# Row maxima of an attention kernel from the high halves alone, two heads at a time in the two halves of the TensorE array

## The reference, cut to what matters

```python
x = L0_attn_x                                   # (4, 1024, 128), float32
x = x + _layernorm(_L0_attn_ref(_layernorm(x), wq, wk, wv, wo))
x = x + _layernorm(_L0_ffn_ref(_layernorm(x), ...))
# _L0_attn_ref, 16 heads of 64:
q, k, v = (einsum('btd,od->bto', x, w) for w in (wq, wk, wv))     # split into heads
q, k = apply_rotary_emb(q, cos, sin), apply_rotary_emb(k, cos, sin)
scores = einsum('bhid,bhjd->bhij', q, k) * 64 ** -0.5
scores = where(causal, scores, -inf)
out = einsum('bhij,bhjd->bhid', softmax(scores), v)
out = einsum('btd,od->bto', out, wo)
```

## Time and profile before

| | |
|---|---|
| median of three runs | 1312.89 us (1311.67 to 1315.08) |
| the profiled execution: its own time, its span | 1314.52 us, 1312.8 us |
| busy in its span: TensorE, VectorE, GpSimd, ScalarE | 1152.0, 994.7, 956.3, 932.3 us |
| granted TensorE clock, mean | 0.956 |

### The profile page before, as it was taken

How to read it: one execution, slowest core, us unless ns; L and a number is a source line. 1 busy time by engine, 2 the same in 40 slices (tenths; PEclk the granted TensorE clock), 3 DMA queues, 4 the chain that set the end, 5 groups by cost and what they waited for, 6 DMA issues and landing times. The chain is left out here.

```text
span 1312.8 us, 34709 instructions
## 1 busy us (share of the span) xinstructions
PE 1152.0 (88%) x13520; PEld 784.5 (60%) x13520; DVE 994.7 (76%) x2153; ACT 932.3 (71%) x2057; POOL 956.3 (73%) x992
## 2 busy tenths in 40 slices
PE   4369999999999999999999899999998398898983
PEld 1126676767766676766666676667776154555551
DVE  7678787878878787878779787877754748787857
ACT  2158878788787878778787878788897665554543
POOL 5439988898887989898888989888675424454524
PEclk8579999999999999999999999999999599999997
DMA  5433515252442515252442515252200400000002
GB/s 178 110 87 76 130 34 130 53 126 73 109 112 52 130 34 131 63 127 66 103 108 55 130 34 130 63 124 72 70 3 2 136 1 1 1 2 0 0 0 64
DMA packets 51147, 95.87 MB, mean 73 GB/s; under 512 B 7088, under 2 KB 23728, under 8 KB 49072
## 3 DMA queue, kind: packets, MB, share of 16 engines
q1 hardware_dynamic: 50992, 93.76, 29.2%
HBM read 56.89 MB, written 33.55 MB: 69 GB/s over the span
## 5 line engine op out<-in xcount | busy, mean ns | idle before, releaser
L652 POOL TENSOR_TENSOR Plo<-P,Phi 128x512 f16<-128x512 f32 (+3 forms) x640 | 537.7, 865 | 139.9 <-ACT P L387 139.3
L384 ACT ACTIVATE Phi<-psS 128x512 f16<-128x512 f32 (+3 forms) x768 | 383.6, 500 | 162.9 <-PE psS L253 114.8
L387 ACT ACTIVATE P<-psS 128x512 f32<-128x512 f32 (+3 forms) x640 | 306.2, 479 | 0.0
L271 PE MATMUL psO<-V,Plo 128*128 128x65 f16 x2304 | 287.8, 194 | 0.0
L267 PE MATMUL psO<-V,Phi 128*128 128x65 f16 x2304 | 287.5, 192 | 0.0
L269 PE MATMUL psO<-V,Phi 128*128 128x64 f16 x2304 | 287.2, 192 | 0.0
L247 PE MATMUL psS<-Q,K 128*128 128x512 f16 (+3 forms) x768 | 251.2, 327 | 38.3 <-DVE Plo L510 32.5
L559 DVE TENSOR_REDUCE pmax<-psX 128x1 f32<-128x512 f32 x384 | 254.3, 682 | 25.8 <-PE psX L328 15.9
L250 PE MATMUL psS<-Q,K 65*128 65x512 f16 (+3 forms) x768 | 251.5, 327 | 0.0
L328 PE MATMUL psX<-K,Q 128*128 128x512 f16 (+3 forms) x768 | 226.5, 330 | 24.2 <-DVE pmax L559 8.5
L267 PEld LDWEIGHTS psO<-V,Phi 128*128 128x128 f16 x2304 | 218.7, 98 | 39.7 <-POOL Plo L652 4.3
(11 more groups left out here) (162 smaller groups left out, 2184.6 us busy)
## 6 DMA issues: line engine op xcount, KB each, us to landing
K<-k_way SPq DMA_DIRECT2D x45, 512.0 KB, 6.9
k_way<-HL SPq DMA_DIRECT2D x60, 256.0 KB, 3.7
q_way<-HL SPq DMA_DIRECT2D x60, 256.0 KB, 4.0
Q<-q_way SPq DMA_DIRECT2D x60, 256.0 KB, 7.1
Q<-q_way SPq DMA_DIRECT2D x15, 512.0 KB, 12.0
x<-in_x SPq DMA_DIRECT2D x4, 512.0 KB, 5.3
out<-x SPq DMA_DIRECT2D x8, 256.0 KB, 2.2
y<-in_x SPq DMA_DIRECT2D x3, 512.0 KB, 10.5
```

The costliest lines, as they stand in the source:

```text
L271: mm = nc.tensor.matmul(O, M.Plo[:, U % NP_, k * P:(k + 1) * P], V[:, HD:2 * HD + 1], start=False, stop=j == t, skip_group_check=True)
L384: nc.scalar.activation(M.Phi[:, U % NP_, 0:w], X, ACT.Exp, scale=SCALE)
L387: nc.scalar.activation(full, X, ACT.Exp, scale=SCALE).then_inc(S.exp_done, 1)
L652: nc.gpsimd.tensor_tensor(M.Plo[:, U % NP_, 0:w], M.P32[:, U % NP_, 0:w], M.Phi[:, U % NP_, 0:w], ALU.subtract).then_inc(S.lo_pool, 1)
```

## The change

The two heads of a pair, 2i and 2i + 1, are worked on together in one call, `maxima`. Each contracts 64 rows: head 2i the rows 0 to 63, head 2i + 1 the rows 64 to 127. For the odd head to have the high halves of its keys in the rows 64 to 127, `K1` of odd heads is laid out the other way round, low halves first. The scores of line 247 add over all 128 rows, and `Q1` holds the same in both halves, so nothing changes for them. The maxima come from the high halves of queries and keys alone. The two matmuls of a piece stand one behind the other and write two banks of `psX`; the masks of both heads follow at the end, still over all 128 rows. A call waits for both banks before it begins. The plan places a pair of items at one step, 18 pairs over steps 8 to 39. The loads of `K1` for odd heads are two transfers of 64 rows each, and there is one semaphore for keys and one for queries of each pair of heads.

```diff
-            for h in range(GH):
-                for k in range(len(MAXB)):
-                    i = h * len(MAXB) + k
-                    put(s, MX_FIRST + i * (MX_LAST - MX_FIRST) // (GH * len(MAXB) - 1) if s >= 0 else MX_EARLY + i,
-                        ("mx", h, k))
+            for i in range(GH // 2 * len(MAXB)):
+                pair, k = divmod(i, len(MAXB))
+                for h in (2 * pair, 2 * pair + 1):
+                    put(s, MX_FIRST + i * (MX_LAST - MX_FIRST) // (GH // 2 * len(MAXB) - 1) if s >= 0
+                        else MX_EARLY + 2 * i, ("mx", h, k))
...
+            def maxima(*pair):
+                s, _, h, k = pair[0]
+                p = (s + 1) % 2
+                if k == 0:
...
+                        pe.wait_ge(S.near_k[h // 2], 48 * (s + 1))
+                        pe.wait_ge(S.near_q[h // 2], 32 * (s + 1))
+                for item in pair:
+                    if number[item] >= NAUX:
+                        pe.wait_ge(S.aux_free[bank(item)], number[item] // NAUX)
+                masks = []
+                c = 0
+                for t, j, n in MAXB[k]:
+                    last = []
+                    for e in range(2):
+                        rows = slice(e * HD, (e + 1) * HD)
+                        X = M.psX[:, bank(pair[e]), :]
+                        last.append(nc.tensor.matmul(X[:, c:c + n * P], M.Q1[rows, p, h + e, t * P:(t + 1) * P],
+                                                     M.K1[rows, p, h + e, j * P:(j + n) * P], start=c == 0,
+                                                     stop=k >= NMIX and j + n - 1 != t, skip_group_check=True))
+                    c += n * P
+                    if j + n - 1 == t:
+                        masks.append(c - P)
+                for e in range(2):
+                    X = M.psX[:, bank(pair[e]), :]
+                    for c in masks:
+                        last[e] = nc.tensor.matmul(X[:, c:c + P], M.ident16[:], M.maskN[:], start=False,
+                                                   stop=c == masks[-1], skip_group_check=True)
+                    last[e].then_inc(S.aux_ready, 1)
...
-                        mm = nc.tensor.matmul(X[:, c:c + n * P], M.Q1[:, p, h, t * P:(t + 1) * P],
-                                              M.K1[:, p, h, j * P:(j + n) * P], start=True, stop=not diagonal)
...
-                            mm = nc.tensor.matmul(X[:, c - P:c], M.ident16[:], M.maskN[:], start=False, stop=True)
...
-                    sp.dma_start(M.K1[:, p, h], krows[:, h]).then_inc(S.near_in[i], 16)
-                    sp.dma_start(M.Q1[0:HD, p, h], qrows[0:HD, h]).then_inc(S.near_in[i], 16)
-                    sp.dma_start(M.Q1[HD:P, p, h], qrows[0:HD, h]).then_inc(S.near_in[i], 16)
+                    sp.dma_start(M.K1[:, p, 2 * i], krows[:, 2 * i]).then_inc(S.near_k[i], 16)
+                    sp.dma_start(M.K1[HD:P, p, 2 * i + 1], krows[0:HD, 2 * i + 1]).then_inc(S.near_k[i], 16)
+                    sp.dma_start(M.K1[0:HD, p, 2 * i + 1], krows[HD:P, 2 * i + 1]).then_inc(S.near_k[i], 16)
+                    sp.dma_start(M.Q1[0:HD, p, h], qrows[0:HD, h]).then_inc(S.near_q[i], 16)
+                    sp.dma_start(M.Q1[HD:P, p, h], qrows[0:HD, h]).then_inc(S.near_q[i], 16)
```

More of the change, by code:

```diff
@@ L273, in weighted @@
                 mm.then_inc(S.weighted_done, 1)
+            def maxima(*pair):
+                s, _, h, k = pair[0]
+                p = (s + 1) % 2
+                if k == 0:
+                    if s < 0:
+                        pe.wait_ge(S.first_k, 16 * 4 * GH)
+                        pe.wait_ge(S.first_q[h // 2], 16 * 2 * GH)
+                    else:
+                        pe.wait_ge(S.near_k[h // 2], 48 * (s + 1))
[22 more added lines that the diff above has]
+                    last[e].then_inc(S.aux_ready, 1)
             def side(item):
@@ L278, in side @@
                 p = (s + 1) % 2
+                if kind == "mx":
+                    if a[0] % 2 == 0:
+                        maxima(item, (s, "mx", a[0] + 1, a[1]))
+                    return
                 if number[item] >= NAUX:
@@ L316, in side @@
                                                   start=i == 0, stop=i == 2)
[L317 to L327, removed]
-                        mm = nc.tensor.matmul(X[:, c:c + n * P], M.Q1[:, p, h, t * P:(t + 1) * P],
-                                              M.K1[:, p, h, j * P:(j + n) * P], start=True, stop=not diagonal)
-                        c += n * P
-                        if diagonal:
-                            mm = nc.tensor.matmul(X[:, c - P:c], M.ident16[:], M.maskN[:], start=False, stop=True)
                 elif kind == "mt":
@@ L715, in first_keys @@
                         sp.dma_start(M.K1[k * HALF:(k + 1) * HALF, 0, h, :],
-                                     M.HL[rows, 0, k, :]).then_inc(S.first_k, 16)
+                                     M.HL[rows, 0, (k + 2 * (h % 2)) % 4, :]).then_inc(S.first_k, 16)
                 for h in range(GH):
@@ L761, in send @@
                     for i in range(2):
-                        sp.wait_ge(S.near_in[i], 48 * (s + 1))
+                        sp.wait_ge(S.near_k[i], 48 * (s + 1))
+                        sp.wait_ge(S.near_q[i], 32 * (s + 1))
                     sp.wait_ge(S.far_in, 32 * (s + 1))
@@ L1463, in build @@
         S.q_out = sem("q_out")
-        S.near_in = [sem(f"near_in{i}") for i in range(2)]
+        S.near_k = [sem(f"near_k{i}") for i in range(2)]
+        S.near_q = [sem(f"near_q{i}") for i in range(2)]
         S.far_in = sem("far_in")
```

## The result

| | before | after |
|---|---|---|
| median | 1312.5 us | 1388.2 us (1383.5 to 1393.5) |
| ratio, 95% interval | | 1.057 (1.053 to 1.062) |
| span of the profiled execution | 1312.8 us | 1385.7 us |

What follows compares the result with a forecast made beforehand. TensorE was taken as the bound, VectorE close behind. Per slot, 36.9 us of work plus 5.8 of waits made 42.7 instead of 43.7; 15 slots saved 15 us, giving 1299 us, range 1275 to 1344.

Steps and rivals of the forecast that it cites:

- The bound: Middle stretch of a slot, 43.7 us: TensorE leads at 42.59 us busy, VectorE 39.02; 3.7 us of waits.
- Overlap: Matmuls of the maxima: two run side by side, starts 0.03 us apart, saving 3.1 us a slot.
- Changes of shape: Maxima calls going from 128 rows to 64 and back, 36 a slot: taken as 0, at most 5.8 us.
- Banks: A pair takes two of three `psX` banks at once: 2.1 us more waits a slot, between 0 and 5.0.
- a bit under half the sum of the worst members: How 2.1 us of bank waits was chosen: six runs of early starts, whose worst members add to 4.8 us.
- the eight operations at step 18: At steps 17 and 18 VectorE's work stacks up: pair, four rope products, pair; no separate size given.
- the five: Cases: as summed 0.44, waits do not grow 0.08, bank waits 0.16, drain at shape changes 0.22, no overlap 0.10.
- Rival 3: Bank waits of pairs eat the saving, deciding at 3.1 us a slot; 1327 us at 4.0 us; chance 0.16.
- rival 4: The array runs empty at each of 36 shape changes, up to 0.16 us each: 1353 us; chance 0.22.
- my worst case, 1384 us: Full drain at shape changes, 1353 us, plus 31 us of bank waits; the two were deliberately not added.
- Loads and layout: SyncE issues 12 transfers a slot instead of 8, same bytes: taken as 0, at most 0.7 us a slot.
- The stage before slot 0: It computes maxima too, but VectorE sets the pace there: no gain or loss was given to it.

Runs made afterwards that it cites:

- alone64: Changed kernel's layout, loads and 64-row matmuls, but one head at a time with the old plan and single bank waits: 1394.7 us, ratio 1.062.
- before_wait2: Kernel before, with each item of the maxima also waiting for the bank after its own: 1388.6 us, ratio 1.058.
- alone128: Kernel before with only the changed kernel's key layout, loads and semaphores; one head at a time over 128 rows: 1312.0 us, ratio 1.000.
- steps_only: Changed kernel with 128-row matmuls, each head waiting only for its own bank and heads of a pair not alternating; plan of pairs kept: 1358.3 us, ratio 1.035.
- pair128: Changed kernel with each matmul of the maxima contracting all 128 rows; pairs, steps and claim of two banks kept: 1384.0 us, ratio 1.053.

## Why the prediction was wrong

- **The bound** was read right: TensorE leads in the maxima's stretch, with VectorE close behind it. 4.1 of the 4.5 us that a slot lost are there. The waits in it were read too high: 3.7 us is what the weight loads stand, and by the starts of the matmuls TensorE lost only 2.4.
- **Overlap** was right in its mechanism. Saved are 3.8 us a slot, not 3.1: the distance of the two starts is mostly 3 to 6 ns, not the 30 that I took from a row of another kind. Here the sentence of the Trainium skill (TensorE: Matmul & The Clock Gate, Part 3), about 4 ns, agrees with the trace.
- **Changes of shape** are the first step that failed. "So I take 0" rested on the 128x32 transposition; 36 changes cost 0.1 us each, 3.5 us, inside the bound of 0.16. The row was of a split by columns, and even after the change that transposition is free in this way, while every change to 64 rows and back is not. The rule of the Trainium skill (TensorEngine Tiling (Array Packing), Key Properties) speaks against the row that I preferred. It gives no price; alone64, with 72 changes, bears out the 0.1 us. Whether the array really runs empty, or the next weights are just not loaded ahead, isn't told apart: a load takes 0.10 us and the gap is 0.10 us.
- **Banks** are the second step that failed: the larger price, 4.4 us a slot, but the smaller error, since 2.1 were forecast and 5.0 given as the most. The mechanism was right and the term mis-sized. What doesn't hold is the halving, "a bit under half the sum of the worst members". That sum, 4.8 us, which is "a run is paid once" taken at its word, is close to what came in the change (4.4 to 5.0) and in before_wait2, whose slots are 4.5 us longer. Nothing but the greater distance between pairs spoke for the half, and it did not help: at steps 9, 18, 21, 26 and 29 a pair, or what follows it, needs an item read that was issued just before, and 3.5 of the 5.1 us there stay with a relieved VectorE. I had seen the eight operations at step 18 and not asked what bank the pair wants there.
- **Which case it was.** None of the five as put. Rival 3 had the mechanism of banks, but set overlap's whole gain against it; rival 4 had the changes, and I refused to add the two, since "a slower TensorE is not ahead of VectorE". Both came, and they add up. That my worst case, 1384 us, lies near the measured 1388 is luck: it took 5.8 us for the changes where 3.5 came, 3.1 for overlap where 3.8 came, and 2.1 for banks where 4.4 came. As to the refusal, the runs speak both ways. With one head at a time the waits did shrink under the changes of shape (2.4 to 0.5 us, alone64); for pairs, no run has changes of shape without overlap, so how their waits would answer to a slower TensorE stays open.
- **The clock** was taken as full in all slots, without a word. Six falls, some 9 us at 1.55 each, came with the change, and no run of mine takes them away alone.
- **Loads and layout**: nothing, as forecast (alone128).
- **The stage before slot 0**: nothing was given to it, and 4.7 us came. It is the claim, by the first load of keys in one profiled execution each: slot 0 begins at 90.49 us before, at 90.78 in steps_only, at 94.88 in pair128 and 95.15 in the changed kernel, and at 96.83 in before_wait2.
- **The last line** is off by 1 us in its own sum: 1299.5 less 1.6 is 1298, not 1299.

The sum with the measured terms: -3.8 + 3.5 + 4.4 = 4.1 us in the stretch, and 0.4 in the rest of the slot. Against the forecast's -1.0 the changes are off by 3.5 us, banks by 2.3, the rest by 0.4 and overlap by 0.7 the other way. Slot 7, from which these numbers are, lies at the upper end of the slots with a full clock.

## What to carry to other kernels

Before two items are joined into one, look up for each joined item which buffer its second half takes and which operation releases it, and how long before this one was issued: with three buffers in rotation a double claim turns "three back" into "two back", and such a claim alone, put into the old kernel at every item of the maxima, cost as much as the whole change. Look also at what comes right ahead of the joined item in the program: an item issued just before is late even when its reader has time to spare. Work in half the rows of the array has its price per change of shape and not per matmul, so it wants more matmuls between two changes; at one pair of 512 columns between them it saves 0.21 us, pays 0.20 and breaks even. Several pairs between two changes were not tried. Where bunching of work is part of a change, give the plan its own run with the arithmetic left as it was.

## What the runs showed of the hardware

- Two matmuls over rows 0 to 63 and 64 to 127, with 512 columns each and different banks of PSUM, mostly start 3 to 6 ns apart and hold up the next matmul hardly longer than one of 64 rows does alone: 0.32 us against 0.31 in alone64, the change of shape included.
- A change from 128 rows to 64 or back costs 0.09 to 0.10 us, and the weight load behind it is not ahead of its matmul. A matmul with 65 rows (L250) is treated as one with 128: it starts 0.16 us behind one of 384 columns and the next 0.17 us behind it (618.51, 618.67, 618.84; the first is L247), with no gap on either side.
- The use of 128x32 of the array costs no such gap: 0.22 us behind 512 columns and 0.11 to the next, before and after the change.
- The granted clock fell from 2.4 to 1.2 GHz in six slots of the changed kernel and in none of pair128 or of the kernel before (slots 0 to 13, behind the start of slot 0); in one fall 16 matmuls took 3.60 us instead of 2.05.
